# Gating GpSimd's edge gathers on steps of the vector engine, in a graph-transformer kernel

## The reference

```
K, Q, V = per-node-type projections of the normalised rows      # (n, 8 heads, 32)
Ks, Qt, Vs = K[src], Q[tgt], V[src]                             # gathered per edge
for t in range(3):                                              # edge types
    scores = sum((Ks @ Wa[t]) * Qt, -1) / sqrt(32) * relation_pri[t]
    w = softmax over all edges of type t, per head
    msgs += where(type == t, w[..., None] * (Vs @ Wm[t]), 0)
agg = segment_sum(msgs, tgt)
```

## Time and profile before

| what | value |
|---|---|
| median of 3 runs | 1098.95 us (1098.5 to 1100.2) |
| span of the profiled execution | 1210.8 us |
| time of the profiled execution outside its span | not recorded |
| edge stage in the profile, first gather to last products | 308.2 to 921.4 us |
| busy share: PE, DVE, ACT, POOL | 79%, 67%, 49%, 53% |
| gathers of the edge stage | 392, mean 948 ns of POOL each |

### The profile page before, as it was taken

One profiled execution on the slowest core, in us unless ns is written; L12 is line 12 of the kernel. 1 busy time (PEld: TensorE's weight loads), 2 busy tenths in 40 slices (PEclk: granted clock), 3 DMA queues, 4 the chain that ended last, 5 costly groups with the idle time before them and its releaser, 6 DMA issues. The chain is left out here.

```text
span 1210.8 us, 18409 instructions
## 1 busy us (share of the span) xinstructions
PE 961.3 (79%) x5315; PEld 679.2 (56%) x5315; DVE 808.0 (67%) x1699; ACT 589.6 (49%) x1532; POOL 638.8 (53%) x821
## 2 busy tenths in 40 slices
PE   5988999999257767777777767767777894999998
PEld 4766777776134434444434434434443893888887
DVE  7743787886256766667766676767765894877451
ACT  2645899983145555455545555555554121322221
POOL 5425777776636656566666666666653005764000
PEclk9998999999567777678777686777777896999999
DMA  9622443444646767666666666666662633210020
GB/s 291 205 74 79 144 141 141 143 141 158 202 122 191 202 185 201 185 189 196 198 185 198 191 195 190 196 195 196 199 180 70 230 93 99 66 58 14 1 87 20
DMA packets 96936, 183.09 MB, mean 151 GB/s; under 512 B 15845, under 2 KB 65580, under 8 KB 96836
## 3 DMA queue, kind: packets, MB, share of 16 engines
q0 software_dynamic: 38896, 129.86, 35.8%
q1 hardware_dynamic: 54660, 48.76, 13.1%
q10 hardware_dynamic: 3280, 3.28, 0.8%
HBM read 147.79 MB, written 34.06 MB: 150 GB/s over the span
## 5 line engine op out<-in xcount | busy, mean ns | idle before, releaser
L1353 POOL DMA_INDIRECT big<-kv_scratch,src_i x392 | 371.7, 948 | 239.0 <-issue 99.3
L1514 PE MATMUL ps<-edge 64*128 64x256 f32 x784 | 169.3, 571 | 66.2 <-ACT edge L1405 56.6
L1633 DVE TENSOR_TENSOR big<-big,ps 128x1024 f32<-128x1024 f32 x98 | 118.8, 1213 | 93.0 <-remote 72.5
L1530 PE MATMUL ps<-big,edge 128*64 128x256 f32 x784 | 148.4, 514 | 29.3 <-issue 18.3
L1514 PEld LDWEIGHTS ps<-edge 64*128 64x128 f32 x784 | 98.2, 271 | 116.0 <-ACT edge L1405 68.8
L1640 DVE TENSOR_REDUCE ps<-big 128x32 f32<-128x1024 f32 x98 | 119.6, 1220 | 0.1
L1530 PEld LDWEIGHTS ps<-big,edge 128*64 128x64 f32 x784 | 66.1, 180 | 91.6 <-issue 73.5
L1692 DVE TENSOR_TENSOR big<-big,ps 128x1024 f32<-128x1024 f32 x98 | 114.9, 1213 | 0.0
L1402 ACT ACTIVATE edge<-ps,iota_n 128x256 f32<-128x256 f32 x98 | 46.1, 470 | 125.6 <-remote 114.6
L1417 ACT ACTIVATE edge<-edge 128x64 f32<-128x64 f32 x392 | 102.9, 334 | 0.0
L1439 ACT ACTIVATE edge<-ps 128x256 f32<-128x256 f32 x98 | 37.3, 381 | 129.7 <-PE ps L1530 84.6
(11 more groups left out here) (338 smaller groups left out, 1873.8 us busy)
## 6 DMA issues: line engine op xcount, KB each, us to landing
edge<-q_scratch SPq DMA_DIRECT2D x196, 64.0 KB
big<-kv_scratch,src_i POOLq DMA_INDIRECT x392
agg_scratch<-big SPq DMA_DIRECT2D x16, 252.0 KB
xn_scratch<-big ACTq DMA_DIRECT2D x5, 640.0 KB, 5.4
mix_scratch<-big SPq DMA_DIRECT2D x25, 128.0 KB
edge<-mix_scratch SPq DMA_DIRECT2D x1, 3200.0 KB, 13.3
big<-xn_scratch SPq DMA_DIRECT2D x25, 128.0 KB, 2.8
edge<-in_x SPq DMA_DIRECT2D x24, 128.0 KB
```

Source lines behind the costliest of these rows:

```text
L1353: pool.indirect_dma_start(kv[:, s, k, :], None, kv_d[0:N, :], bass.IndirectOffsetOnAxis(ap=src_i[:, e:e + 1], axis=0)).then_inc(got[s], 16)
L1514: ins = pe.matmul(qr_ps[g % 2][:, (2 * hg + k) * D:(2 * hg + k + 1) * D], ohT[64 * hg:64 * hg + 64, g % 2, k * P:(k + 1) * P], qwin[64 * h ...
L1530: ins = pe.matmul(sums_of(g)[64 * hg:64 * hg + 64, :], oneh[:, s, k, hg * 64:hg * 64 + 64], kv[:, s, 2 * hg + k, D:2 * D], start=(k == 0), ...
L1633: dve.tensor_tensor(k_rows, k_rows, qr_ps[g % 2].rearrange("p (k d) -> p k d", d=D), ALU.mult).then_inc(pr, 1)
```

## The change

POOL's gathers are now issued in pairs, and each pair first waits for a step of DVE. With `b = g // 2 - 1`, the batch ahead of the one that is gathered for, the first pair of an even group waits for `products(2b)`, its second pair for `head_sums(2b)`, the first pair of the odd group for `head_sums(2b+1)`, and its second pair for `messages(2b-2)`. The ring's wait on `yd` stays. Nothing else differs: the same gathers go into the same slots, and all other engines run the same instructions.

```diff
             @block.gpsimd
             def _(pool):
+                def pace(g, half):
+                    b = g // 2 - 1
+                    if g % 2 == 0 and half == 0:
+                        at_least(pool, pr, 2 * b + 1)
+                    elif g % 2 == 0:
+                        at_least(pool, sc, 2 * b + 1)
+                    elif half == 0:
+                        at_least(pool, sc, 2 * b + 2)
+                    else:
+                        at_least(pool, ms, 2 * b - 1)
+
                 def rows_of(g):
                     s = g % RING
                     at_least(pool, yd, g - RING + 1)
                     for k in range(EG):
+                        if k % 2 == 0:
+                            pace(g, k // 2)
                         e = EG * g + k
                         pool.indirect_dma_start(kv[:, s, k, :], None, kv_d[0:N, :],
```

## The result

The changed kernel takes 1140.91 us (1139.9 to 1143.41, 4 runs) beside 1099.58 us (1098.5 to 1101.93, 4 runs) of the kernel before. The ratio is 1.0389, with a 95% interval of 1.0359 to 1.0419. That is 41 us slower; the forecast was 17 us slower.

A forecast was written before the change was run, and what follows sets the result against it. POOL's gather issuing was taken to bound the edge stage, at 10.17 us per batch. A loop of 10.50 us added 15.5 us over 47 batches and the start 2, so 1098.95 + 17.5 gave 1116 us, range 1097 to 1134.

The forecast's parts named there:

- The bound: Edge stage before the change: POOL's gather issue rate bounds it, 1.25 us a gather, 10.0 us for eight.
- The loop: From one odd group's products to the next through head sums, gate, issues and landing: 10.50 us per batch against 10.17.
- The stops: DVE's "remote" waits in the edge stage, 113.4 us: taken to belong to the profiled execution, not the timed runs.
- DVE's end to POOL's start: Term between DVE's head sums and the odd group's first gather on POOL: 0.09 us.
- Last issue to products: Term from POOL's last odd-group gather issue to the start of the products it releases: 3.96 us.
- The even group: Its two gated pairs in the edge stage: gathers land 0.8 us early and cost nothing.
- Met waits: Waits on POOL's gathers that are already satisfied: priced at 0, at most 0.1 us each.
- The wait of `subtract` on PE: Sign in the profile after: DVE's wait there, 33.0 us before, should shrink because products come later.
- The start: Opening of the edge stage, where POOL now waits for the first products: 2 us lost, once.
- Much slower: Rival: the wait on PE stays, or the even group's room is used up; loop 11.1 us, 1143 us; chance 0.08.
- No change: Rival: landing in 3.4 us or less, or PE holding DVE at 10.4 us per batch; about 1099 us; chance 0.21.
- Faster: Rival: timed runs have stops too, caused by the flood of gathers; 1061 us if half were there; chance 0.12.

The follow-up runs named there:

- e16: Kernel before, with one memset of 256 elements per partition on POOL ahead of each gather: 1171.4 beside 1098.05 us, ratio 1.0664.
- e10: Changed kernel with only the wait on head sums at the odd group's first pair left: 1140.77 us, 1.0389 of the kernel before.
- e15: Changed kernel with all four waits kept but each met one batch earlier, without stops: 1099.77 us, 1.0001 of the kernel before.
- e12: Kernel before, with one tiny memset on POOL ahead of each gather, without stops: 1098.52 us, 1.0004 of the kernel before.
- e1: Changed kernel with all four waits kept but each met one batch earlier, with stops: 1.0006 of the kernel before.
- e8: Changed kernel with the ring's wait and the wait on DVE's step in the other order, with stops: 1.084 of the kernel before.
- e14: Changed kernel without the odd group's first-pair wait on head sums, other three waits kept, without stops: 1112.95 us, 1.0119 of the kernel before.
- e11: Changed kernel with the odd group's first pair waiting for products of the same group instead of head sums: 1108.25 us, 1.0069 of the kernel before.
- e5: Changed kernel without any edit, run where there are stops: 1313.41 beside 1214.14 us for the kernel before, 1.0839.
- e9: Changed kernel with the ring's wait and the wait on DVE's step in the other order, without stops: 1124.68 beside 1099.88 us, 1.0237.
- e13: Kernel before, with two tiny memsets on POOL ahead of each gather: 1101.29 us, 1.0006 of the kernel before.

## Why the prediction was wrong in size

**The bound was right.** POOL's issuing, 1.25 us a gather, bounds the stage before (e16). The loop through the odd group's gate bounds it after, and that one gate alone gives the whole cost (e10), while no wait costs anything by being there (e15).

**The stops.** I took them to belong to the profiled execution. For the runs against which the change was timed, leaving them out was right: e12 gives 10.04 us per batch, and I had worked out 10.17 from the difference of two sums. As a statement on the stops it was too strong: in e1 to e8 the timed runs of the kernel before took 1214 to 1216 us, as long as the profiled execution with stops. What makes them come is open.

**The step that failed** is the term "DVE's end to POOL's start: 0.09 us". I read it from an ordinary POOL instruction, not from a gather behind a separate wait instruction, though the printed order of the changed program showed two waits on just this gather. It measured 0.74 us in the batch shown and 0.75 as the mean, 0.66 more than the term, which is 31 us over 47 batches. The row from another instruction was no bound for it.

The other terms of the loop held. Products to head sums' end: 2.70 forecast, 2.62 measured. Four issues: 3.75, the same. Last issue to products: 3.96 forecast, 4.08 in the batch shown and 3.87 as the mean. The loop came out at 10.99 instead of 10.50: 0.66 more by the release, 0.17 less by the two others.

The second, smaller error is the base. I took 10.17 us per batch; e12, counted in the same way from odd group to odd group, has 10.09. The stops had taken 600.00 - 482.10 = 117.9 us out of the window of 48 batches and not 111.85. Loop and base together, (0.49 + 0.08) x 47 = 27 us, with the forecast's 17.5 make 44. Without the 2 us that I had put down for the start they make 42, near the 41 measured.

**The even group** cost nothing in the changed kernel, as forecast: e10, without its two gates, is no faster. But its room was 0.3 us, not the 0.8 that I had: its last issue stood 4.20 us ahead of its products as the mean, where a gather took 3.87. And once the odd group's gate is gone or earlier, the even group's gate on products costs some microseconds (e14, e11). **Met waits** at 0 was right (e15). **The wait of `subtract` on PE** fell to 1.3 us, but it is only 3.4 us without stops and without the change (e12), so this sign says little. **The start** cost nothing that can be told from the measured 41 us: 47 steps of 10.99 - 10.09 = 0.90 us are 42 already.

**The rivals.** "Much slower" gave 1143, close to what was measured, but by another mechanism. It needed the wait on PE to stay in the loop, and that wait was 1.3 us in the whole stage, or the even group to close the loop, and that group's products waited for a gather in 2 of 47 batches. So its nearness is luck. "No change" fell with the landing, 3.87 us where it needed 3.4, and its other condition, timed batches of 10.4 us, with e12's 10.04. The 2.6 us of the Trainium skill ("DMA: Bandwidth & Descriptors", section "Anatomy of one DMA — SWDGE (gpsimd) path") did not show here; the shortest of the 47 landings took 3.46. "Faster", that gating would calm the stops, fell too: in e5 the gate made the case with stops worse, 1.0839.

My range ended at 1134 because I widened only the landing and left the release at its single row.

## What to carry to other kernels

A prefetch gated on its consumer's progress closes a loop: gate, issue, landing, use, gate. Sum it, and compare it with what bounds the stage; one batch of distance cost 41 us here and two cost nothing, with the same waits. Where an instruction needs two waits, put the one that comes last on the instruction itself. And price a release from the same kind of instruction, or leave it a wide range.

## What was not expected of the hardware

- A gather behind a separate wait instruction that was just released started 0.75 us after DVE's end; with that wait on the gather itself it was 0.27 us (changed kernel, e9; 0.75 also behind products in e11 and e14). When the waits had been met long before, neither showed (0.30 us between gathers, e15).
- Two memsets of 0.11 us fit between two gathers at no cost (e13), one of 0.33 us, with a wait on the one before it, cost 0.19 us (e16).
- In some groups of runs the kernel before lost about 115 us to common stops in the edge stage (308 to 921 us against 308 to 806 in e12), and in others nothing. In the changed kernel the stops cost more (1313 against 1141 us). The record gives one chip number for e5 to e8, which had them, and e10 to e12, which had none, so the chip alone doesn't seem to decide. Whether recording causes them is open.
